# First attention stage of a two-layer decoder: a softmax's maximum and subtraction over 16 heads at once instead of 8 and 8

## The reference

```python
def _causal_attn(q, k, v):                       # 16 heads of 8 channels
    scores = jnp.einsum('bthd,bshd->bhts', q, k) * scale
    scores = jnp.where(mask, scores, -jnp.inf)
    attn = jax.nn.softmax(scores, axis=-1)
    return jnp.einsum('bhts,bshd->bthd', attn, v)
...
ctx = _causal_attn(q, k, v)
q2 = conv1d(ctx, conv_w, padding 1) + conv_b
ctx2 = _causal_attn(q2, k, v)
out = ctx2 @ out_w.T + out_b
...
x = _layernorm(x + out)
```

## Time and profile before

| what | value |
|---|---|
| median of 3 runs | 3978.86 us (3962.93 to 3979.88) |
| the profiled execution, its own time | 3980.16 us |
| its span, first to last instruction | 3977.9 us |
| first stage, first to last maximum | 62.9 to 724.5 us |
| busy share of the whole span | PE 70%, DVE 61%, POOL 47%, ACT 40% |
| mean granted TensorE clock | 0.877 of full speed |

### The profile page before, as it was taken

One profiled execution on the slowest core, in us unless ns is written; L12 is line 12 of the kernel. 1 busy time (PEld: TensorE's weight loads), 2 busy tenths in 40 slices (PEclk: granted clock), 3 DMA queues, 4 the chain that ended last, 5 costly groups with the idle time before them and its releaser, 6 DMA issues.

```text
span 3977.9 us, 93960 instructions
## 1 busy us (share of the span) xinstructions
PE 2801.2 (70%) x28526; PEld 1944.6 (49%) x28529; DVE 2445.7 (61%) x6828; ACT 1588.0 (40%) x3994; POOL 1863.6 (47%) x2306
## 2 busy tenths in 40 slices
PE   3999999758888888882058879999999930266600
PEld 2666666435555555551036656666666620255500
DVE  2777777528878878884001148888888860155545
ACT  2666666424545545541013335555555510011100
POOL 4222222006766666663730036666666617411177
PEclk9999999978989989985579989999999965699955
DMA  2111111351111111111222211111111102211133
GB/s 52 42 41 39 39 41 44 117 172 42 50 47 49 48 48 49 47 32 34 77 71 74 67 39 30 30 28 30 29 30 30 26 11 78 64 55 55 54 85 87
DMA packets 282379, 207.17 MB, mean 52 GB/s; under 512 B 61731, under 2 KB 246456, under 8 KB 281905
## 3 DMA queue, kind: packets, MB, share of 16 engines
q1 hardware_dynamic: 262960, 164.88, 14.1%
q0 software_dynamic: 19200, 39.62, 3.7%
HBM read 114.99 MB, written 90.18 MB: 52 GB/s over the span
## 4 chain that ended last, share of the span: by engine, by line
issue 21%; PE 14%; POOL 13%; DVE 5%; POOLq 0%; ACT 0%; DMA 0%; DVEq 0%; ACTq 0%; SPq 0%
PE scores_ps L1049 3%; POOL k_bd L2001 2%; POOL rows L2053 2%; POOL shared L2152 2%; POOL shared L2001 2%; POOL got L2098 2%; PE heads_ps L1056 1%; PE desk_ps L1056 1%; PE scores_ps L1167 1%; POOL norm_rstd L1997 1%; PE scores_ps L1169 1%; PE heads_ps L1167 1%; DVE e_T L1821 1%; PE desk_ps L1167 1%; POOL rstd L2160 1%
## 5 line engine op out<-in xcount | busy, mean ns | idle before, releaser
L1997 POOL TENSOR_TENSOR norm_rstd<-norm_veps,minus_half 128x1 f32<-128x1 f32 x384 | 218.3, 569 | 380.6 <-DVE norm_veps L1557 374.8
L2053 POOL DMA_INDIRECT rows<-e_in,slot_put x256 | 248.9, 972 | 164.0 <-issue 107.4
L1278 ACT ACTIVATE probs<-probs 128x512 f32<-128x512 f32 x384 | 239.9, 625 | 107.6 <-DVE probs L1577 107.2
L1575 DVE TENSOR_REDUCE row_max<-scores_ps 128x8 f32<-128x512 f32 x384 | 261.9, 682 | 26.0 <-issue 16.1
L1577 DVE TENSOR_TENSOR probs<-scores_ps,row_max 128x512 f32<-128x512 f32 x384 | 265.4, 691 | 13.2
L1282 ACT ACTIVATE turned<-scores_ps 128x512 f32<-128x512 f32 x384 | 228.1, 594 | 109.2 <-PE scores_ps L907 103.5
L907 PE MATMUL scores_ps<-consts,probs 128*128 128x128 f32 x1536 | 243.1, 282 | 7.3 <-ACT probs L1278 6.5
L1210 ACT ACTIVATE probs<-probs 128x512 f32<-128x512 f32 x256 | 161.4, 630 | 141.4 <-DVE probs L1496 138.5
L1494 DVE TENSOR_REDUCE row_max<-scores_ps 128x8 f32<-128x512 f32 x256 | 174.7, 682 | 57.0 <-PE scores_ps L763 57.0
L2142 POOL TENSOR_TENSOR o_rstd<-o_veps,minus_half 128x2 f32<-128x2 f32 x72 | 49.9, 693 | 288.7 <-DVE o_veps L1926 288.7
L907 PEld LDWEIGHTS scores_ps<-consts,probs 128*128 128x128 f32 x1536 | 176.2, 143 | 16.0 <-ACT probs L1278 9.8
(11 more groups left out here) (335 smaller groups left out, 8327.6 us busy)
## 6 DMA issues: line engine op xcount, KB each, us to landing
hop_dram<-shared SPq DMA_DIRECT2D x64, 256.0 KB, 2.1
hop_in<-hop_dram SPq DMA_DIRECT2D x64, 256.0 KB, 3.0
rows<-zero_rows SPq DMA_DIRECT2D x64, 144.0 KB, 1.9
shared<-rows SPq DMA_DIRECT2D x72, 128.0 KB, 2.1
moe<-shared SPq DMA_DIRECT2D x72, 128.0 KB, 1.8
rows<-zero_rows SPq DMA_DIRECT2D x64, 128.0 KB, 1.8
c_in<-in_ctx SPq DMA_DIRECT2D x128, 64.0 KB, 1.9
c_two<-in_ctx SPq DMA_DIRECT2D x128, 64.0 KB, 2.4
```

Of the source, the lines that this page charges most:

```text
L1278: act.activation(half, half, ACT.Exp, scale=scale).then_inc(at.exped.sem, 1)
L1575: dve.tensor_reduce(best, sc, AX, ALU.max).then_inc(at.shift.sem, 1)
L1997: pool.tensor_tensor(n_rstd[:, k, u, :], n_veps[:, k, u, :], minus_half[:, 0:1], ALU.pow).then_inc(sig.sem, 1)
L2053: pool.indirect_dma_start(out=rows, out_offset=bass.IndirectOffsetOnAxis(ap=slot_put[:, c, U * n + i:U * n + i + 1], axis=0), in_=put_rows ...
```

## The change

`softmax1` loses its loop over the two halves. One maximum reads all 1024 scores of a row across both banks and writes 16 numbers, one wait follows, and one subtraction reads the 1024 scores and writes all of `probs[a]`. The maximum raises `sub_ready` by 1 and the subtraction by 3, so that the count after a softmax is `4n + 4` as before; both waits of ACT, for `4n + 2` and `4n + 4`, are met by the subtraction's one step. Nothing else is edited: ACT still takes the exponential in two halves, and PE still transposes in two halves.

```diff
             def softmax1(a, n):
                 dve.wait_ge(sc_ready[a], n + 1)
-                for g in range(NR):
-                    sc = scores_ps[:, a, g, :].rearrange("p (h t) -> p h t", t=S)
-                    best = row_max[a][:, 8 * g:8 * g + 8]
-                    dve.tensor_reduce(best, sc, AX, ALU.max).then_inc(sub_ready[a], 1)
-                    dve.wait_ge(sub_ready[a], 4 * n + 2 * g + 1)
-                    dve.tensor_tensor(probs[a][:, 512 * g:512 * g + 512].rearrange("p (h t) -> p h t", t=S), sc,
-                                      best.unsqueeze(2).broadcast_to([P, 8, S]), ALU.subtract)\
-                       .then_inc(sub_ready[a], 1)
+                sc = scores_ps[:, a].rearrange("p g (h t) -> p (g h) t", t=S)
+                dve.tensor_reduce(row_max[a], sc, AX, ALU.max).then_inc(sub_ready[a], 1)
+                dve.wait_ge(sub_ready[a], 4 * n + 1)
+                dve.tensor_tensor(probs[a].rearrange("p (h t) -> p h t", t=S), sc,
+                                  row_max[a].unsqueeze(2).broadcast_to([P, H, S]), ALU.subtract).then_inc(sub_ready[a], 3)
```

## The result

The changed kernel takes 4194.73 us (median of 4 runs, 4189.51 to 4202.28) against 3979.24 for the kernel before, measured beside it: a ratio of 1.0566, 95% interval 1.0546 to 1.0586. It is 215 us slower, where 145 were forecast. The sign was right; the time lies 25 us over the end of the range.

The account below looks back on a forecast made before the run. The first stage was taken as bound by a three-leg chain across engines, 10.21 us a tile. To the profiled 3980.16 us it added 127 for the longer period and 18 for the clock: 4125, forecast as 4124 us, range 4085 to 4170.

Parts of the forecast that it names:

- The cost of the wide operations: Maximum and subtraction on DVE over 1024 columns: 1.22 us each, 0.53 us more for the second 512 columns.
- the sum: The first stage's period added up from its three legs: 2.52 + 4.60 + 5.10 = 12.22 us a tile against 10.21.
- DVE saves: Two DVE instructions less per softmax: 2.38 us in place of 2.64, saving 0.26 us, twice a tile.
- Leg 1: Softmax 0's maximum to ACT's exponential of half 0: grows by 1.07 us, from 1.45 to 2.52.
- leg 2: From ACT's first exponential through copies, POOL's spread and rstd, and DVE's x_out to softmax 1: stays 4.60 us.
- Leg 3: Softmax 1 back to softmax 0: DVE's 4.16 us replaced by 5.10 through exponential, PE's transposes, mask and next scores.
- The first rival: Scores' path does not end the way back to softmax 0: 11.02 us a tile, +51 us, 4030 us; chance 5%.
- The new period: First-stage tile takes 12.22 us against 10.21: +2.01 us, over 63 intervals +127 us.
- The clock: PE's busy share falls from 91% to 76% in the first stage; low clock in 11.5 tiles costs 18 us.
- The upper bound: Clock cost in the first stage if PE's whole 9.28 us stretch to 16.2 in the low-clock tiles: 46 us.
- The signs named beforehand: Expected in the first stage's profile: 12.2 us a tile, DVE waiting 1.2 us before softmax 0, clock 0.9 to 0.99.
- The clock stays low: Most of the first stage at 1.2 GHz, PE needing 16.2 us a tile: +377 us, 4356 us; chance 5%.

Follow-up runs that it names:

- Order exchanged: Changed kernel with PE's scores of the next softmax 0 put ahead of the transposes of softmax 1's first half: 4037.16 us, ratio 1.0151.
- the run with filled waits: Changed kernel with six unused bf16 matmuls on PE ahead of the transposes of softmax 1's first half: 4111.69 us, ratio 1.0341.
- softmax 0 alone: Kernel before with only softmax 0 in one piece, softmax 1 still in halves: 4072.87 us, ratio 1.0239.

## Why the prediction was right in sign and short in size

- *The cost of the wide operations*: right, 1220 and 1225 ns. The chain pays 0.07 us more than the sum each time: maximum to subtraction is 1.31 to 1.33 us start to start (463.31 and 470.04 in the trace of after, to 464.62 and 471.37), not 1.24 to 1.26. DVE saves 0.18 us a softmax, not 0.26 (464.62 to the next instruction at 465.77 is 1.15; 1.31 + 1.15 = 2.46).
- *Leg 1, late handover; leg 2, unchanged*: right, 7.18 us against 7.12.
- *Leg 3 passes from DVE to the path over PE's queue*: right. Order exchanged, it is back at 3.97; clock held, it is 5.19 against 5.10. The first rival (only leg 1 grows) was wrong as given, and is what the exchanged order makes true: 4037 measured, 4030 worked out.
- *The new period at full clock*: 12.37 us against 12.22, so 63 x (12.37 - 10.24) = 134 us against 127.
- *The clock*: this step failed. The prediction took the mean busy share of PE, found a stretch with a similar one (clock 0.91), and spread 18% of low time evenly over the tiles: 11.5 tiles at 1.53 us, 18 us. Measured are 52 of 60 tiles with all or nearly all of the path at 1.2 GHz: 63 x (13.67 - 12.37) = 82 us, 90 by the run with filled waits. The price of one such tile was right (1.53 us; the way back is 6.73 against 5.19, 1.54). The count was wrong: in the changed kernel the clock does not fall at random places in a tile but in PE's long wait (51 of 52 falls), and the change had put that wait directly ahead of the stretch that the chain runs over. With that wait filled the clock held. The upper bound (46 us) had the same fault, since it scaled a price and kept the count.
- *The signs named beforehand*: DVE's wait before softmax 0 was 2.4 us a tile on average, not 1.2, and the clock of the stage 0.84, not 0.9 to 0.99. The prediction had said that a clock under 0.85 would make the size wrong and not the sign, which is what happened. The result lies where its rival "The clock stays low" had 5%, but not by that rival's mechanism: PE would have been busy all the time, and it is busy 489 of 600 us.
- *Total*: 134 + 82 = 216 from the legs, 215 measured.
- *The mean share as a guide* fails on its own too. In the same 600 us PE is busy 507.81 and 508.21 us at a clock of 1.00 (order exchanged; waits filled), but 512.90 us at 0.95 (softmax 0 alone). More busy time, lower clock (part of the 512.90 is the low clock itself, at which PE's instructions take longer).
- The Trainium skill's advice on splitting ("Perfetto Trace Analysis", Optimizing Scalar/DVE Operations), set beside the sum, pointed the right way: with DVE unsaturated, one operation in place of two left bubbles on ACT and PE.

## What to carry to other kernels

Two halves that a consumer takes one by one are a pipeline, not overhead: before fusing them, add up what the first consumer's later start does to everything queued behind it on every engine, the work of other tiles first. Where a wait of TensorE ends up on the chain, price what follows it at the low clock for every period as the upper bound (with a wait of 1.3 us or more the clock fell in 26 to 52 of 60 tiles here), not by the mean clock of a stretch with a like busy share. And look at a wait that recurs once a period for a small instruction standing behind a large one it has nothing to do with: moving `rstd` ahead of the spread gave 0.6% where saving DVE time gave nothing. Look afterwards at what the moved instruction now runs beside: here `x_out` became five times as long.

## What was not expected of the hardware

- The granted clock fell in a wait of PE of 1.33 us (0.68 in it, 0.50 in the 3.39 us behind it), tile after tile, although PE had worked 1.53 of the 1.54 us before (ahead of these lay a wait of 0.58 us). With the wait at 0.35 us the mean over 600 us is 1.00.
- A wait alike in length need not have this effect each time: with softmax 1 alone in one piece the clock fell in 30 of 60 tiles, in the changed kernel in 52. Nor is so long a wait needed: with softmax 0 alone it fell in 24 tiles, whose longest waits are 0.85 us and, before the transposes, 0.19; with waits of 0.85 and 0.13 (order exchanged) or 0.85 and 0.35 (waits filled) it never fell in the 60 tiles. What decides between them was not settled; the periods differ, and no run changed that alone.
- A small DVE instruction beside POOL's spread of the keys lasted until that spread had ended: `x_out`, 0.40 us elsewhere, took 2.05, 0.81 or 1.51 us in the four runs where the two overlap, and ended 0.08 us behind the spread in all but one of the 236 cases between 100 and 700 us (0.09 there). What holds it was not tried.
- An operation that waits for the result of the one before it started 0.07 us later than the sum from 512 columns gave. Why was not tried.
